# A graph-network kernel in which TensorE waits for destination one-hots once per tile of four subtiles instead of once per subtile

## The reference, cut to what matters

```python
x = _layernorm(x + _L0_gnn_ref(x, src, dst))                      # segment_sum(x[src], dst)
x = _layernorm(x + _L1_gnn_ref(x, edge_weight, src, dst, 10))     # ten rounds of a segment_max
x = _layernorm(x + _L2_gnn_ref(x, edge_index, edge_weight, ...))  # three recurrent layers
x = _layernorm(x + _L3_gnn_ref(x, edge_index, ...))               # edge MLP, mean over dst
```

```python
def gcn(x, W, b):
    xw = x @ W
    agg = jax.ops.segment_sum(nw[:, None] * xw[src], dst, num_segments=n)
    return agg + b
```

## Time and profile before

| | |
|---|---|
| time, median of 3 runs | 8579.5 us (8568.05 to 8579.87) |
| time of the profiled execution | 8566.12 us |
| its span, first to last instruction | 8564.4 us |
| PE busy (matmuls) | 6111.6 us, 71% of the span |
| DVE busy | 6750.9 us, 79% |
| ACT busy | 3629.1 us, 42% |
| first layer's additions on PE | 1495.8 to 1974 us |
| recurrent layers' additions on PE | 6167.5 to 7373.9 us |

### The profile page before, as it was taken

How to read it: one execution, slowest core, us unless ns; L and a number is a source line. 1 busy time by engine, 2 the same in 40 slices (tenths; PEclk the granted TensorE clock), 3 DMA queues, 4 the chain that set the end, 5 groups by cost and what they waited for, 6 DMA issues and landing times. The chain is left out here.

```text
span 8564.4 us, 139046 instructions
## 1 busy us (share of the span) xinstructions
PE 6111.6 (71%) x42018; PEld 3076.7 (36%) x42018; DVE 6750.9 (79%) x10765; ACT 3629.1 (42%) x4488; POOL 2258.3 (26%) x2014
## 2 busy tenths in 40 slices
PE   2111013878989798888989898989698989656665
PEld 2101012344434343443434343434354545323332
DVE  8999778767889888888889898989787979744443
ACT  0133000224656565555656565656344444233333
POOL 0000000001333333324233332424200000277775
PEclk9999999999999999999999999999899999777777
DMA  2000000886767676666767676767576767311111
GB/s 87 3 0 0 22 5 20 296 286 212 251 211 254 204 244 211 230 227 220 241 214 249 210 251 210 253 204 254 186 285 224 292 225 290 120 22 29 26 29 25
DMA packets 450936, 1460.71 MB, mean 171 GB/s; under 512 B 79869, under 2 KB 115365, under 8 KB 383008
## 3 DMA queue, kind: packets, MB, share of 16 engines
q1 hardware_dynamic: 228922, 1119.71, 38.3%
q10 hardware_dynamic: 157440, 298.89, 9.7%
q0 software_dynamic: 63872, 32.83, 2.2%
HBM read 1159.47 MB, written 291.94 MB: 169 GB/s over the span
## 5 line engine op out<-in xcount | busy, mean ns | idle before, releaser
L1465 PE MATMUL acc<-dst_hot,parts 128*128 128x512 bf16 x11600 | 2936.6, 382 | 336.4 <-issue 321.9
L1524 ACT ACTIVATE parts_out<-acc 96x1024 bf16<-96x1024 f32 x2320 | 2364.6, 1019 | 1722.1 <-PE acc L1476 1712.4
L1340 DVE TENSOR_SCALAR dst_hot<-dst_rows,node_f 128x2048 bf16<-128x2048 int16 x2910 | 2050.9, 739 | 120.2 <-PE acc L1476 109.9
L1428 POOL DMA_INDIRECT group_best<-best_dram,best_row x1250 | 1406.6, 1125 | 2696.1 <-SPq L1391 2401.4
L1465 PEld LDWEIGHTS acc<-dst_hot,parts 128*128 x11600 | 1048.7, 97 | 1547.8 <-issue 665.8
L993 POOL DMA_INDIRECT gathered<-table_dram,source_index x719 | 822.3, 1144 | 1529.5 <-POOLq L158 1310.7
L1476 PE MATMUL acc<-source,parts 128*128 128x128 bf16 x9280 | 910.2, 221 | 118.9 <-DMA source<-source_dram 115.6
L1476 PEld LDWEIGHTS acc<-source,parts 128*128 x9280 | 623.1, 98 | 762.6 <-issue 313.8
L1553 DVE TENSOR_TENSOR_SCAN best<-joined,best,risen 128x512 f32<-128x512 uint8 x570 | 727.6, 1276 | 0.7
L1547 DVE SCALAR_TENSOR_TENSOR risen<-rise,factor 128x512 f32<-128x512 f32 x580 | 400.9, 691 | 377.9 <-PE rise L1488 354.0
L360 PE MATMUL turned<-identity,ping 128*128 128x128 f32 x224 | 55.1, 428 | 771.7 <-DVEq L449 771.7
(11 more groups left out here) (378 smaller groups left out, 8269.9 us busy)
## 6 DMA issues: line engine op xcount, KB each, us to landing
dst_rows<-step_dst_dram SPq DMA_DIRECT2D x291, 1024.0 KB, 4.6
source<-source_dram SPq DMA_DIRECT2D x291, 1024.0 KB, 7.2
dst_kept_in<-dst_hot_dram SPq DMA_DIRECT2D x174, 1280.0 KB, 5.7
best_dram<-best_out ACTq DMA_DIRECT2D x580, 256.0 KB
factor<-step_weight_dram ACTq DMA_DIRECT2D x560, 256.0 KB
sources<-source_dram SPq DMA_DIRECT2D x174, 512.0 KB, 6.6
dst_hot_dram<-dst_kept SPq DMA_DIRECT2D x58, 1280.0 KB, 5.5
src_rows<-step_src_dram SPq DMA_DIRECT2D x58, 512.0 KB, 7.3
```

Source lines behind the costliest of these rows:

```text
L1340: nc.vector.tensor_scalar(hot[k % 2][b][:, :], index_rows[k // 2 % 2][:, k % 2, :], node_f[:, b:b + 1], None, ALU.is_equal).then_inc(hot_r ...
L1428: pool.indirect_dma_start(group_best[:, g, h, :], None, best_dram, bass.IndirectOffsetOnAxis(ap=best_row[:, i:i + 1], axis=0)).then_inc(en ...
L1465: nc.tensor.matmul(acc[n % 3][:, 0:TILE], blocks[b], hot[k % 2][b][:, q * TILE:(q + 1) * TILE], start=(b == 0), stop=(b == DST_BLOCKS - 1))
L1524: act.activation(moved[n % (2 * QUADS)][:, :], acc[n % 3][0:SPLIT, :], ACT.Copy).then_inc(tile_moved, 1)
```

## The change

PE waits on `hot_ready` only before the first subtile of a tile, and then for the last one-hot of that tile. In the first layer this is subtile j = 3's (four one-hots made by DVE per tile); in the recurrent layers it is subtile j = 2's (two made per tile). The number of one-hots, their order on DVE, their buffers and every other wait stay as they are.

```diff
 KEPT_SUBS = tuple(range(1, STEP_SUBS, 2))
 MADE_SUBS = tuple(i for i in range(STEP_SUBS) if i not in KEPT_SUBS)
+MADE_IN_TILE = len(MADE_SUBS) // QUADS
@@ first layer, PE
                                     i = q * SUBS + j
                                     n = c * STEP_SUBS + i
-                                    pe.wait_ge(hot_ready, n + 1)
+                                    if not j:
+                                        pe.wait_ge(hot_ready, n + SUBS)
                                     nc.tensor.matmul(to[0], found[c % 2][:, i, :], one_hot_of(n)[:, 0:BANK], start=False, stop=False)
@@ recurrent layers, PE
                                             n = c * len(MADE_SUBS) + MADE_SUBS.index(i)
-                                            pe.wait_ge(hot_ready, n + 1)
+                                            if not j:
+                                                pe.wait_ge(hot_ready, n + MADE_IN_TILE)
                                             one_hot = dst_hot[n % HOTS2]
```

## The result

| kernel | median | runs | range |
|---|---|---|---|
| before | 8579.7 us | 4 | 8568.05 to 8587.33 |
| after | 8774.4 us | 4 | 8767.59 to 8782.88 |

The ratio is 1.0229, with an interval of 1.0211 to 1.0246: 194.7 us slower. The forecast was 8756 us, with a range of 8705 to 8790. The profiled execution of after took 8767.59 us, with a span of 8765.8 us.

What follows compares the result with a forecast made beforehand. First layer bound by PE's own queue, register work and slow loads; recurrent layers by a PE, ACT and DVE loop. 0 + 178 on 8566.1 gave 8744, 8757 on the median's scale; predicted 8756 us, range 8705 to 8790.

Steps and rivals of the forecast that it cites:

- The first layer, costed at 0: First layer, three waits removed per tile: DVE's one-hots are ahead, PE's own queue binds, so sum 0.
- A wait already met costs nothing: PE's removed waits: asking for a semaphore that is already met was costed at nothing.
- The recurrent chain, step by step: Recurrent layers, PE to ACT to DVE: held tiles lengthen each step from 6.35 to 7.41 us, +178 us in all.
- Moved one-hot 10: DVE, recurrent step: one-hot 10 comes after the cast and stage 4, so is ready 0.37 us later, at 6666.08.
- unmoved one-hot 6: DVE, recurrent step: one-hot 6 hangs on stages 1 and 2 and doesn't move; tile 1 starts at 6664.25.
- three holds: PE, recurrent step: held at j = 0 of tiles 0, 1 and 2, some 0.4, 0.4 and 0.3 us long.
- the tile time of 1.43: PE, recurrent layers: a tile takes 1.43 us from j = 0 to the next gather, also after a hold.
- step 1: Recurrent tile 0: j = 0 waits for one-hot 2 until 6662.23, and the next gather moves by 0.37 us.
- its bounds: Recurrent layers' loss: from +0.75 us per step (+126 us) to +1.2 us per step (+202 us).
- The role of the load: PE, recurrent layers: after a hold the queue still has the load of the next tile's numbers and all arithmetic to do.
- rival B: PE's queue works on under a hold in the recurrent layers: +0.31 us per step, +52 us, 8632 us; chance 0.05.
- Where the idle time lies: DVE, recurrent layers: its idle time should lie before stage 0, about 1 us per step.

Runs made afterwards that it cites:

- The half alone: The kernel before with only the first layer changed to wait once per tile, recurrent layers as before: 8574.1 us, ratio 1.0005.
- early one-hots: Even one-hots of the recurrent layers made one place earlier on DVE: on the changed kernel 8570.4 us (1.0000), on the kernel before 8539.3 us (0.9966).

## Why the prediction was right

*The first layer, costed at 0.* Right. The half alone measured 1.0005, its stage is 477 us for 478, and the idle time stayed, at 57.5 us in the changed kernel, under another label.

*A wait already met costs nothing.* Right to what can be told: three waits less in each of 58 x 4 = 232 tiles, 696 in all, and the ratio's interval is 0.9993 to 1.0016.

*The recurrent chain, step by step.* Times from stage 0, forecast and then measured in the step above:

| event | forecast | after |
|---|---|---|
| tile 0, j = 0 | 1.17 | 1.23 |
| next gather | 2.60 | 2.73 |
| ACT's move | 2.99 | 3.12 |
| cast | 3.37 | 3.50 |
| tile 1, j = 0 | 3.19 | 3.19 |
| stage 4 | 4.03 | 4.16 |
| next gather | 4.62 | 4.66 |
| tile 2, j = 0 | 5.07 | 5.20 |
| next gather | 6.50 | 6.61 |
| stage 0 | 7.41 | 7.52 |

The chain is the one foreseen. Moved one-hot 10, unmoved one-hot 6, three holds, none in tile 3, and 0.91 us from the last gather to stage 0 are as put down; so is the tile time of 1.43, with 1.50, 1.47 and 1.41 in this step and 1.47, 1.43 and 1.44 on average.

*The term that was mis-sized* is step 1, the hold of tile 0: the forecast let the gather move by 0.37 us, and it moved by 0.50 (2.73 for 2.23). PE went on 0.12 us after one-hot 2 was ready, where 0.05 was taken from the hold at subtile 6, and the tile took 1.50 us. Those 0.13 us go through ACT, the cast and one-hot 10 to stage 0 nearly whole. On average over the 21 whole steps of the stretch it is 0.10: ACT's move behind that gather starts 3.09 us after stage 0, where the forecast has 2.99, and the step is 7.52 us where it has 7.41. So the step lengthened by 1.18 (1.17 in the single step shown) and not 1.06. With 168 steps that is 198 us for 178, and 201 was the growth of the stage; between the medians it was 195. The forecast lay 18 us low, within its bounds (up to 1.2 us per step, +202).

Part of the slow release can be read from the trace of after:

```profile
L1754 PEldq EVENT_SEMAPHORE  x174: 51/51/51, 6168.0 to 7571.3; - x174
```

L1754 is the wait for `hot_ready`. It stands as an instruction of its own, 0.051 us long, once per step (174 = 3 x 58): in tile 0, whose first matmul also waits for `message_ready`. In the step above it runs from 6840.63, between the one-hot's end (6840.59) and the weight load (6840.71). In tiles 1 and 2 the matmul carries the wait. In all 22 steps read the release in tile 0 takes 0.12 us. The forecast took its 0.05 us from a hold of the other kind.

*The role of the load,* that after a hold it is still to do, was right and decided against rival B; its size was only seen when the load was moved. The Trainium skill (Perfetto Trace Analysis, Tensor Engine Instruction), by which the sequencer is free while a matmul waits in the wait queue, isn't borne out here: in tiles 1 and 2, where the matmul carries the wait, the load behind it starts with the release, and moving it ahead of the wait gave back 102 us, which by that rule would be nothing.

*Where the idle time lies* was half wrong: the forecast put DVE's about 1 us per step before stage 0. It is split, 0.42 us there, 0.73 before stage 4 and 0.35 before stage 7, in the step shown. The cast became later by 0.50 us, not 0.37 (the same 0.13).

*What stays open.* No run took the separate wait instruction of tile 0 away, so that it costs the 0.05 us is read and not tested. Of the 0.22 us that the short hold costs with early one-hots, 0.03 isn't traced to a place; all of it goes away with the load ahead of the wait. And no run shows why the loads of tile numbers are slow in the first layer (median 0.65 us for 0.30): the share of busy DMA engines is nearly the same in both stretches, 0.84 and 0.79.

## What to carry to other kernels

Before waits are merged into one, ask what their producer has in hand at that moment: with seven subtiles in hand the merge is free; where PE already waits for two one-hots in each step, it adds the time to the last one-hot, and all of the queue's work behind the wait moves with it. What the queue has to do for later work (a register load here) belongs ahead of a wait that really holds; ahead of one that doesn't it gained nothing. The sizes of single holds don't add in a loop between engines (316 us singly, 195 together): walk one step and see what each hangs on.

## What the runs showed of the hardware

A label can outlive its cause. In the first layer 55.5 us of idle time stood as waiting for one-hots; with three of four waits removed, 57.0 us of it stood as "issue", and the time hadn't moved.

The granted clock differed in a stretch where it made no difference. In the stage before the first layer, which the change doesn't touch, before and then after:

```profile
500.00:1480.00 980.00, 160.62 (x1168) 134.34 (x1166) 829.97 (x1149) 152.73 (x147) 0.00 (x0) 1.00 0.02 6
```

```profile
500.00:1480.00 980.00, 159.17 (x1168) 133.53 (x1168) 829.94 (x1150) 153.28 (x147) 0.00 (x0) 0.51 0.02 6
```

The granted clock is 1.00 in one and 0.51, about the lower level of 1.2 GHz, in the other, at the same 16% of PE work and the same length. It lowers the whole kernel's mean clock (0.932 and 0.878), which could be taken for the cause of the loss. It isn't: the kernel before ran at both mean clocks with no such difference (8579.4 us at 0.877 and 8569.2 at 0.933 in one series). In the recurrent layers it was 0.96 before and 0.97 after:

```profile
6167.00:7374.00 1207.00, 1127.93 (x8483) 604.90 (x8482) 1042.70 (x2372) 534.42 (x1079) 0.00 (x0) 0.96 0.71 262
```

```profile
6167.00:7576.00 1409.00, 1235.51 (x8479) 624.96 (x8480) 1048.04 (x2370) 533.69 (x1079) 0.00 (x0) 0.97 0.61 224
```

DVE and ACT do the same work in both (1043 and 1048, 534 us); only the time around it grew. PE's busy time grew too, 1128 to 1236 us, although it has the same number of matmuls, 8480. These are not longer: their records add up to 2354.8 us before and 2356.5 after. But a stretch in which two records overlap is counted once in busy time, and matmuls that are held apart overlap less. A higher busy time of PE is here a sign of a worse filled array.
